# A vision tower on one NeuronCore: routed part with folded affine and padded tiles, keys placed by slot through four DMAs, one product for four heads

## The reference, cut to what matters

```
h = tok(x)                                        # 196 tokens, 192 dimensions
h = h + attn(layernorm(h))                        # 12 heads, causal, relative term in the keys
h0 = layernorm(h)                                 # hidden_states of the routed block
normed = ln(h0) * g1 + b1
scores = sigmoid(normed @ Wr + br)                # one number a token
idx = the k tokens of least score                 # k = 29 of 196
attn_out = softmax_heads(normed@Wq, normed@Wk) (normed@Wv) @ Wo + bo
pooled = sum(scores / sum(scores) * normed)
mix_out = (normed + scores * pooled) @ Wm + bm
m = h0 + where(token in idx, attn_out, mix_out)
h = h + m + gelu((ln(m) * g2 + b2) @ W1 + bf1) @ W2 + bf2      
```

## Time and profile before

| | us |
|---|---|
| median of 3 runs | 7143.11 |
| lowest, highest | 7137.82, 7144.05 |
| profiled execution, its time | 7138.35 |
| profiled execution, its span | 7136.6 |
| one image in the loop | 54.61 |

### The profile page before, as it was taken

One profiled execution on the slowest core, in us unless ns is written; L12 is line 12 of the kernel. 1 busy time (PEld: TensorE's weight loads), 2 busy tenths in 40 slices (PEclk: granted clock), 3 DMA queues, 4 the chain that ended last, 5 costly groups with the idle time before them and its releaser, 6 DMA issues.

```text
span 7136.6 us, 158568 instructions
## 1 busy us (share of the span) xinstructions
PE 6388.1 (90%) x51392; PEld 5565.0 (78%) x51392; DVE 5387.4 (75%) x15934; ACT 3645.2 (51%) x12160; POOL 3458.2 (48%) x4559
## 2 busy tenths in 40 slices
PE   4999999999999999999999999999999999999998
PEld 4777777777777777777777777777777777777777
DVE  3777777777777777777777777777777777777776
ACT  1555555554555555555555554555555555555554
POOL 4444444445444444444444445444444444444443
PEclk8888888888888888888888888888888888888887
DMA  4211121112112111211121112112111211121110
GB/s 47 30 22 23 22 29 22 23 25 27 23 22 27 24 23 22 29 22 23 22 29 22 23 25 27 23 22 27 24 23 22 29 22 23 22 29 22 23 25 8
DMA packets 228657, 175.82 MB, mean 25 GB/s; under 512 B 27785, under 2 KB 228126, under 8 KB 228630
## 3 DMA queue, kind: packets, MB, share of 16 engines
q1 hardware_dynamic: 218934, 173.46, 18.6%
q10 hardware_dynamic: 8336, 1.07, 0.2%
q0 software_dynamic: 1360, 0.96, 0.2%
HBM read 156.11 MB, written 19.27 MB: 25 GB/s over the span
## 4 chain that ended last, share of the span: by engine, by line
issue 28%; PE 21%; POOL 19%; DVE 18%; POOLq 9%; DVEq 3%; ACT 1%; ACTq 0%
POOL p L503 10%; PE bank L693 8%; DVE qz L1109 5%; POOL rstd L486 4%; PE bank L645 4%; DVE negmax L1128 2%; DVE z L1062 2%; PE bank L681 2%; POOLq L556 2%; POOL h L557 2%; POOLq L485 2%; PE bank L781 2%; POOL res L565 2%; PE bank L792 2%; POOLq L582 2%
## 5 line engine op out<-in xcount | busy, mean ns | idle before, releaser
L1514 ACT ACTIVATE p<-bank,negmax 98x98 f32<-98x98 f32 (+1 forms) x3072 | 1132.9, 376 | 318.8 <-DVE negmax L1128 275.8
L503 POOL TENSOR_TENSOR p<-p,rden 98x294 f32<-98x294 f32 (+1 forms) x1024 | 947.4, 950 | 610.9 <-DVE rden L1142 610.9
L1522 ACT COPY pT<-bank 98x392 f32<-98x392 f32 x768 | 374.2, 488 | 1304.4 <-PE bank L714 1297.4
L693 PE MATMUL bank<-tokw,x_sb 128*98 128x193 f32 x4096 | 988.4, 403 | 9.1 <-DVEq L1049 9.1
L693 PEld LDWEIGHTS bank<-tokw,x_sb 128*98 128x98 f32 x4096 | 874.4, 263 | 80.6 <-issue 29.2
L1128 DVE TENSOR_REDUCE negmax<-bank 98x1 f32<-98x196 f32 (+2 forms) x1536 | 627.3, 457 | 324.4 <-PE bank L681 324.2
L714 PE MATMUL bank<-ident,p 98*98 98x98 f32 x4608 | 727.8, 319 | 106.2 <-DVE y_row L1161 101.8
L714 PEld LDWEIGHTS bank<-ident,p 98*98 98x98 f32 x4608 | 561.8, 166 | 283.8 <-issue 140.4
L681 PE MATMUL bank<-qk_parts,qz 128*98 128x196 f32 (+1 forms) x6144 | 744.8, 266 | 0.0
L681 PEld LDWEIGHTS bank<-qk_parts,qz 128*98 128x98 f32 x6144 | 657.0, 166 | 11.4
L520 POOL TENSOR_TENSOR qz<-qk_parts,ones 32x588 fp32r<-32x588 f32 x256 | 301.1, 1176 | 722.1 <-DVE qk_parts L1099 701.8
(11 more groups left out here) (271 smaller groups left out, 15081.2 us busy)
## 6 DMA issues: line engine op xcount, KB each, us to landing
x_sb<-in_x SPq DMA_DIRECT2D x384, 196.0 KB, 4.8
x_sb<-in_x SPq DMA_DIRECT2D x384, 189.0 KB, 7.9
out<-out_row SPq DMA_DIRECT2D x128, 147.0 KB
x_store<-in_L_tok_W SPq DMA_DIRECT2D x6, 96.0 KB
stage<-in_L_ffn_W SPq DMA_DIRECT2D x1, 576.0 KB
gstore<-in_L_ffn_W SPq DMA_DIRECT2D x1, 384.0 KB
p<-in_L_attn_w_attn ACTq DMA_DIRECT2D x2, 96.0 KB
gstore<-in_L_ffn_W ACTq DMA_DIRECT2D x1, 192.0 KB
```

The source lines that it names most:

```text
L503: last = gp.tensor_tensor(heads, heads, rden[:, s, t].unsqueeze(2).broadcast_to([HT, NG, w]), ALU.mult)
L693: mm(bank[b][0:HT, t * (D + 1):(t + 1) * (D + 1)], xf[:, a:a + (HT - 1) * PS + 1:PS], tokw[:, q], start=t == 0 and q == 0, stop=q == QH - ...
L1514: sc.activation((p1 if t else p0)[0:HT, 3 * s + g], bank[b][0:HT, c0:c0 + (T if t else HT)], ACT.Exp, bias=negmax[:, s, t, g:g + 1], accum ...
L1522: sc.copy(pt_dst(name[0], int(name[1:])), bank[RING[name]][0:HT, 0:4 * HT]).then_inc(sem["pT_act"], 1)
```

## The change

The queries are no longer spread; the keys are. Four transfers on SP copy, for each slot s, 32 partitions of `khi` and `klo` into `kz[:, part, s]`, which is zero elsewhere (set once). A matmul then has the plain `qparts` as stationary operand and streams four heads at 98 columns, or two at 196. There are nine score units, `S0` to `S8` (three for each group g of four heads), in place of eight, and heads are numbered by group. Keys are made before queries, and the ring of banks is new. In the routed block, g1 and b1 are folded into the weights once; the mixing branch takes `mrow = z @ Wm'` on PE ahead of the gather, the sigmoid is computed on 98 x 2 values instead of rows spread over 128 partitions, the pooled row comes from a PE product of `sig` and `mrow` (`weighted_sum`), and `mixed` is made on DVE from it. `keep`, `fbm` and `f0` are added on POOL; `f0` itself is made on ACT (`block_input`). Ranks take two DVE operations in place of four. Several matmul operands are padded with zeros to 128 partitions or to 66 columns.

```diff
-RING = dict(S0=0, S1=1, S2=2, T0=3, S3=0, S4=1, S5=2, S6=0, S7=1, A0=2, A1=0, A2=3, B0=1, A3=2,
-            B1=0, A4=1, A5=3, B2=0)
+RING = dict(S0=0, S1=1, S2=2, T0=3, S3=0, S4=1, S5=2, S6=0, S7=1, S8=2, A0=0, A1=1, B0=3, A2=2,
+            A3=0, B1=1, A4=3, A5=2, B2=0)
...
+            def place_keys(n):
+
+                sp.wait_ge(sem["klo_sb"], after("klo_sb", n))
+                for s in range(4):
+                    at = slice(32 * s, 32 * s + 32)
+                    sp.dma_start(kz[at, :, s].bitcast(F32),
+                                 qk_parts[at, 0:2].bitcast(F32)).then_inc(sem["kz_in"], 16)
...
-                    for i in (2, 3):
-                        at = slice(32 * i, 32 * i + 32)
-                        gp.drain()
-                        if i == 2:
-                            gp.wait_ge(sem["qparts_sb"], after("qparts_sb", n))
-                        gp.tensor_tensor(qz[at, i], qparts[at].bitcast(F32),
-                                         ones[at, 0:1].unsqueeze(2).broadcast_to([32, NG, T]),
-                                         ALU.mult).then_inc(sem["qz2_sb"], 1)
...
-                    gp.wait_ge(sem["sel_sb"], after("sel_sb", m))
-                    gp.tensor_tensor(f1[:], both(fbm), keep[:].unsqueeze(2).broadcast_to(
+                    gp.wait_ge(sem["mixed_sb"], after("mixed_sb", m))
+                    gp.tensor_tensor(f1[:], mixed[:], both(fbm), ALU.add)
+                    gp.drain()
+                    gp.tensor_tensor(f1[:], f1[:], keep[:].unsqueeze(2).broadcast_to(
                         [HT, 2, D]), ALU.mult)
                     gp.drain()
+                    gp.wait_ge(sem["f0_sb"], after("f0_sb", m))
                     gp.tensor_tensor(f1[:], f1[:], f0[:], ALU.add).then_inc(sem["f1b_sb"], 1)
...
+                    gp.tensor_tensor(nmean[:], mv_f[:, :, 0], r, ALU.mult)
+                    gp.drain()
+                    gp.tensor_tensor(shift[:], nmean[:], neg1[:], ALU.mult).then_inc(sem["shift_sb"], 1)
...
+                    group_cols(2, split["wk"], "k_mm")
                     group_cols(0, split["wq"], "q_mm")
-                    group_cols(2, split["wk"], "k_mm")
...
-                    for i, (g, t, c0) in enumerate(heads):
-                        w = T if t else HT
-                        for part in (khi, klo):
-                            last = mm(bank[b][0:HT, c0:c0 + w],
-                                      qz[:, s, g, HT * t:HT * t + HT], part[:, g, 0:w],
-                                      start=False, stop=i == len(heads) - 1 and part is klo,
-                                      skip_group_check=True)
+                    for part in range(2):
+                        last = mm(o, qparts[:, g, HT * t:HT * t + HT],
+                                  kz[:, part, slots[0]:slots[-1] + 1, g, 0:w], start=False,
+                                  stop=part == 1, skip_group_check=True)
...
-                            pe.wait_ge(sem["klo_sb"], after("klo_sb", n))
+                            pe.wait_ge(sem["qparts_sb"], after("qparts_sb", n))
+                            pe.wait_ge(sem["kz_in"], after("kz_in", n))
...
+                    pe.wait_ge(sem["mixed_sb"], after("mixed_sb", m))
...
-                def mix():
-                    pe.wait_ge(sem["mTs_sb"], after("mTs_sb", m))
-                    cols_to_rows(7, mTs, split["fwm"], "mix_mm")
+                def mixing_rows():
+
+                    if front:
+                        pe.wait_ge(sem["v_sb"], after("v_sb", n))
+                    cols_to_rows(4, nTs, split["fwm"], "mrow_mm")
+
+                def weighted_sum():
+
+                    pe.wait_ge(sem["mrow_sb"], after("mrow_sb", m))
+                    pe.wait_ge(sem["sig_sb"], after("sig_sb", m))
+                    for t in range(2):
+                        last = mm(bank[4][0:HT, 0:D + 1], sig[:, t:t + 1].broadcast_to([HT, HT]),
+                                  mrow[:, t], start=t == 0, stop=t == 1)
+                    last.then_inc(sem["usum_mm"], 1)
...
-        onesr = sb("onesr", [64, T], F32R)
-        bqparts = sb("bqparts", [64, NG * 128], F32R)
+        onesr = sb("onesr", [128, T], F32R)
+        bqparts = sb("bqparts", [128, NG * 128], F32R)
-                        last = mm(bank[6][0:SELP, 0:D], cols(ctxT, chunk), cols(fwo, chunk),
+                        last = mm(bank[6][0:66, 0:D], ctxT[:, chunk], fwo[:, chunk],
-                                  selT[0:NSEL, HT * t:HT * t + HT], ao[0:NSEL], start=True,
+                                  selT[:, HT * t:HT * t + HT], ao[:], start=True,
```

More of the change, by code:

```diff
@@ L1030, in _ @@
+            ve.drain()
+            ve.tensor_scalar(nbr[:], br[0:HT], -1.0, None, ALU.mult)
+            ve.drain()
+            ve.tensor_scalar(limits[:, 0:1], nbr[:], TOPZ, None, ALU.add)
+            ve.tensor_scalar(limits[:, 1:2], nbr[:], -88.0, None, ALU.add)
+            for chunk, (lo, hi) in enumerate(KC):
+                size = hi - lo
+                ve.tensor_scalar(fbqs[0:size, chunk:chunk + 1], fbq[0:size, chunk:chunk + 1], QSCALE,
                                  None, ALU.mult)
-            ve.tensor_tensor(bf1[:], bf1[:], bank[4][:, 0:F // 128], ALU.add)
+            for name in folded:
+                ve.tensor_copy(split[name][:, 0::2], raw[name][:])
@@ L1182, in routing_scores @@
                     ve.wait_ge(sem["score_mm"], after("score_mm", m))
-                    ve.tensor_scalar(zrow[:], bank[6][:, 0:T], br[:], None,
-                                     ALU.add).then_inc(sem["z_sb"], 1)
+                    ve.tensor_scalar(zclip[:], bank[6][0:HT, 0:T], limits[:, 0:1], limits[:, 1:2],
+                                     ALU.min, ALU.max)
+                    ve.drain()
+                    for t in range(2):
+                        last = ve.tensor_tensor_reduce(
+                            scr[0:HT, t, 0:HT], zclip[:, HT * t:HT * t + HT], ident[0:HT, 0:HT],
+                            1.0, 0.0, ALU.mult, ALU.add, zi[:, t:t + 1])
@@ L1249, in mix_cols @@
-                def mix_cols():
-                    ve.drain()
-                    split_cols(mTs, mT, "mTs_sb")
+                    for t in range(2):
+                        last = ve.scalar_tensor_tensor(mixed[:, t], bank[4][0:HT, 0:D],
+                                                       wmix[:, t:t + 1], mrow[:, t, 0:D],
+                                                       ALU.mult, ALU.add)
+                    last.then_inc(sem["mixed_sb"], 1)
                 def q_blocks():
@@ L1525, in exp_scores @@
                 def exp_scores():
[L1526 to L1527 removed]
+                    sc.wait_ge(sem["zi_sb"], after("zi_sb", m))
+                    sc.activation(ez[:], zi[:], ACT.Exp, bias=nbr[:], scale=-1.0).then_inc(
+                        sem["expz"], 1)
                 def keys_values2():
@@ L1567, in mlp_cols_hi, with block_input @@
                     cols_hi(z3Ts, 6, "z3_T", m, "z3T_sb")
+                def block_input():
+                    sc.wait_ge(sem["h2_sb"], after("h2_sb", n))
+                    sc.wait_ge(sem["shift_sb"], after("shift_sb", n))
+                    for t in range(2):
+                        last = sc.activation(f0[:, t], h2[:, t], ACT.Identity,
+                                             bias=shift[:, t:t + 1], scale=vf[:, 1, t:t + 1])
+                    last.then_inc(sem["f0_sb"], 1)
                 def gelu(j):
```

395 lines of the change are left out of this document (188 added, 207 removed).

## The result

The changed kernel takes 6867.83 us (median of 4 runs, 6865.77 to 6878.51), beside 7141.23 us for the kernel before: a ratio of 0.962, 95% interval 0.9604 to 0.9637. An image of the loop takes 52.50 us on average where it took 54.61. The forecast had 7095 us and 54.2: the direction was right and the size was not. An image gained 2.1 us where 0.4 was forecast, five times as much.

What follows compares the result with a forecast made beforehand. PE was taken as the bound, through about 5 us of waits an image and a granted clock of 0.87. Six stages summed to 54.67 us against 54.61, less 0.5: 54.2, -50 us over 126 passes, 7095 us; range 6780 to 7330.

Steps and rivals of the forecast that it cites:

- The padded queries: Query products ahead of the first scores: with a padded bias, queries go at the keys' pace, -0.93 us an image.
- the sum: Six stages of PE in an image, added from the z transposes on: 54.67 us against 54.61 before.
- The keys: Ahead of the first scores: four SP transfers land at 8.7 us behind the z transposes, between bounds 7.5 and 9.7.
- the prediction's own sign: At the first scores: a gap over 1 us released by the transfer means the late-keys rival is at work.
- the rival of the late keys: Transfers land at 10, not 8.7; PE stands 1.9 us, low clock costs 1.5: 57.0 an image, 7445 us; chance 0.12.
- The other new waits: PE waits 3.25 us for `A1` and 1.05 for `mixed`; scaling of the context +0.85; z3's chain within 4.2.
- The scores: Nine score units in place of eight: 5.32 us becomes 4.4, with long streams a little better, -1.1 an image.
- This takes the clock as falling at once when PE stops for `A1`: Low clock from `A1` on is priced in the 54.67; a later fall saves up to 1.8 us, 0.5 taken off.
- The fast rival: Clock comes back or never falls in the later half, perhaps through padding: 49.3 an image, 6475 us; half, 6790; chance 0.13.
- The clock that stays low up to the projection: Attention's stage stays 4.93 us, the projection costs about 0.9 more: 55.8 an image, 7295 us; chance 0.23.

Runs made afterwards that it cites:

- a_nopad: Changed kernel with the product behind the routed context and the scatter taken back to unpadded shapes (32 columns, 29 rows): 7065.66 us.
- a_fill_nopad: a_fill with the product behind the routed context and the scatter taken back to unpadded shapes: 6703.48 us.
- b_pad: Kernel before, with only the ones and the query bias padded from 64 to 128 rows: 7140.93 us.
- a_fill: Changed kernel with 28 unused full-size products into a free bank in PE's wait ahead of `A1`: 6580.44 us.
- a_max2: Changed kernel with DVE taking the maxima of the routed scores ahead of those of `S7`: 6699.24 us.
- a_usum6: Changed kernel with the weighted sum in bank 6 instead of bank 4, so the routed scores no longer wait for `mixed`: 6698.12 us.
- a_both: Changed kernel with the weighted sum in bank 6 and the maxima of the routed scores ahead of those of `S7`: 6696.83 us.
- b_fill: Kernel before, with unused full-size products in two waits: 9 ahead of the ranks, 18 ahead of the mixing branch: 6714.76 us.
- b_fill18: Kernel before, with only the 18 unused products in the mixing branch's wait, none ahead of the ranks: 6721.52 us.
- a_keys2: Changed kernel with two of the four key transfers issued by ACT instead of SP: 6839.56 us.

## Why the prediction was right or wrong

- **What bounds the kernel, right and too narrow.** PE's waits and the clock. The forecast took the clock for an effect of the waits; a_nopad and a_fill_nopad show that padding two products changes it with the waits left as they are.
- **The padded queries, right in size** (-0.93 forecast, -0.86 in b_pad). The prediction set this against the Trainium skill, "TensorE: Matmul & The Clock Gate", section on loading the stationary operand, by which the number of rows does not matter to a load's time. The two do not clash: the trace agrees with the section (184 ns for 64 rows, 194 for 128), and the padding removes idle time between loads. The forecast then let the gain pass into the sum, and alone in the kernel before it was worth 0.
- **The keys, 0.3 too early.** SP issued at 4.2 (4.3 forecast), but its four issues took 2.53 us where 1.97 was priced, and the last landing came at 9.0, between the two bounds. The prediction's 8.05, an estimate from the Trainium skill, "DMA: Bandwidth & Descriptors", section on the anatomy of one DMA, was a microsecond early; that section gives its fit for transfers issued by GpSimd, and these are SP's. PE was ready at 7.8, not 8.15. By the prediction's own sign (a gap over 1 us ended by the transfer) the rival of the late keys was at work, but in small: the wait was 1.23 us and not 1.9, and no low clock followed it.
- **The other new waits, right**: places, releasers and, where a size was given, the size to 0.2 us.
- **The scores.** 4.4 was worked out for nine units and came: 0.58 and twice 0.44 a group. The further 0.2 put into the -1.1 for long streams did not.
- **The failed step: the low clock was priced too high.** It is the step "This takes the clock as falling at once when PE stops for `A1`", with 1.2 GHz from there to the attention, less 0.5. The rival in which the clock comes back put the low terms at 1.05, 1.5, 0.8 and 2.0, so the forecast held 5.35 - 0.5 = 4.85 us an image for the clock. The images of a_fill at full clock show 52.5 - 49.6 = 2.9 in its place. The difference is 1.95, and the shortfall of the forecast is 54.2 - 52.5 = 1.7. At full clock the sum gave 49.3, measured 49.6; part of that closeness is luck, since misses of up to 0.5 in single stages (20.9 forecast and 20.4 measured up to the end of the routed transposes, 4.2 and 4.65 to the MLP transposes) offset each other.
- **Why too dear.** In length, 13 us were taken for every image and 10.2 came on average; that is half of the 1.95. In price, the forecast had 0.37 us for each us of low clock. Measured it is 0.25 (before, 3.4 over 13.65), 0.28 (after, 2.9 over 10.2) and 0.27 (a_nopad less after). Even the 43 images with 13.65 us of it are only 3.8 us longer than those of a_fill at full clock. Two things in the rows keep the price down: the wait for the context's scaling is 0.76 at either clock, and the stage to the MLP transposes does not shrink at full clock (4.65 us in a_fill, 4.41 after, by the forecast's boundary), since the wait for z3 grows from 0.90 to 1.48 us (after, then a_fill):

```profile
4082.88 0.56 PE L643 MATMUL bank<-ident,f 98*128 98x98 f32 x4 [0.90 <-DVE f L1112]
```

```profile
4064.18 0.56 PE L643 MATMUL bank<-ident,f 98*128 98x98 f32 x4 [1.48 <-DVE f L1118]
```

- **The fast rival** ("if that is enough activity") had 0.13 and named the padding as the mechanism; half of it gave 6790. a_nopad shows that mechanism at work: it was under-weighted, the standstill of 3.1 us having been taken as decisive.
- **The clock that stays low up to the projection** did not come: the longest stretches end 41 us into the image, just ahead of the attention. The Trainium skill, "TensorE: Matmul & The Clock Gate", part on the PE transpose, was cited for it; here the clock rose at 4072.3 behind 3.3 us with 20 matmuls, about 16 of them transposes, so the trace does not agree.
- **Where the gain came from.** Held at full clock the two kernels take 51.2 and 49.6: 1.6 of the 2.1 us an image is less work and less waiting, 0.5 a smaller price of the clock. No run takes back the placing of the keys, the folding of g1 and b1 or the new mixing branch by itself, so the share of each is known only as far as the stages separate them.

What stays open is why so many kernels come to the same image on average: b_pad and before to 54.61, and a_max2, a_usum6, a_both and a_fill_nopad to 51.20, with different waits and different work. Image and clock seem to keep step, so that a small gain at one place is returned by a low stretch at another; this is not shown beyond b_pad, and no run here tells what would set the step. The 51.18 of b_fill, which has no low clock to return anything by, may be chance.

## What to carry to other kernels

Price an edit twice, at full clock and by what it does to the clock, and read the granted clock after every edit: here 0.86 us of saved work an image was worth nothing alone, and unused products in two waits were worth 5.9%. Filling a wait of PE with full-size products into a free bank delayed nothing here by more than 0.1 us, and tells at once how much of a time is the clock's. In these kernels, which also wait, a us of low clock cost 0.25 to 0.28 us an image, where 0.37 had been forecast.

## What was not expected of the hardware

- The clock fell during the unpadded scatter with no wait over 0.8 us near it (a_fill_nopad, 7.2 us an image low). With the padded one it stayed up throughout in 27 of the 112 images of a_fill, and for all but 2.7 us an image on average.
- A standstill of 1.23 us (keys) was not followed by low clock. One of 0.96 (ranks) was in every image of the kernel before, and hardly ever in b_fill18, where only the other wait had been filled.
- A bias product of 64 rows among products of 128 cost 0.29 us more than one of 128 rows (b_pad: 0.86 over three), though its load is no longer.
- Two queues instead of one brought the last of 588 KB of keys in only 0.3 us sooner (a_keys2).
